# Moving a layer norm's statistics and its application between units of an attention pipeline

## The reference, cut to what matters

```python
x = x + attn(layernorm(x), wq, wk, wv, wo)   # x: (4, 256, 256), 4 sequences of 256 tokens
x = x + ffn(layernorm(x), W1, W2, W3)
# layernorm: (x - mean) / sqrt(var + 1e-5), over the last axis
# attn: 16 query heads, 4 key/value heads of 128, rotary embedding (rope) on q and k,
#       causal scores times a decay exp(-lambda_h * lag), no softmax, then wo
# ffn:  silu(x W1^T) * (x W3^T), Walsh-Hadamard transform over 1024 hidden, then W2
```

## Time and profile before

| | before |
|---|---|
| runs | 272.18 us median of 3 (272.09 to 272.81) |
| the profiled execution | 272.2 us, span of its instructions 270.4 us |
| mean granted TensorE clock | 0.998 |
| busy: PE / DVE / ACT / POOL | 263.1 / 205.5 / 168.0 / 146.1 us |

### The profile page before, as it was taken

One profiled execution on the slowest core, in us unless ns is written; L12 is line 12 of the kernel. 1 busy time (PEld: TensorE's weight loads), 2 busy tenths in 40 slices (PEclk: granted clock), 3 DMA queues, 4 the chain that ended last, 5 costly groups with the idle time before them and its releaser, 6 DMA issues.

```text
span 270.4 us, 4196 instructions
## 1 busy us (share of the span) xinstructions
PE 263.1 (97%) x1498; PEld 228.0 (84%) x1498; DVE 205.5 (76%) x331; ACT 168.0 (62%) x283; POOL 146.1 (54%) x106
## 2 busy tenths in 40 slices
PE   8999799999999999999999999999999999999995
PEld 6686678988889898888889889898888879988895
DVE  2799999999879897959899799795576983143333
ACT  2988977985798767556867768984353542043230
POOL 2306999988879467532795897899519200000000
PEclk9999999999999999999999999999999999999999
DMA  5595422220220000000010002200000000100002
GB/s 185 187 354 176 167 80 80 78 78 0 80 71 10 0 1 0 4 0 0 2 59 18 2 4 73 78 5 0 2 0 2 0 0 23 57 0 0 2 0 78
DMA packets 5491, 13.23 MB, mean 49 GB/s; under 512 B 608, under 2 KB 2272, under 8 KB 5472
## 3 DMA queue, kind: packets, MB, share of 16 engines
q1 hardware_dynamic: 5184, 12.65, 13.5%
q10 hardware_dynamic: 288, 0.33, 0.3%
HBM read 11.93 MB, written 1.05 MB: 48 GB/s over the span
## 4 chain that ended last, share of the span: by engine, by line
PE 79%; DVE 15%; issue 3%; ACT 2%; POOL 0%; DVEq 0%; POOLq 0%
PE bank L312 25%; PE bank L313 24%; PE bank L314 24%; PE bank L335 3%; DVE rope_b L973 2%; DVE bank L1000 2%; PE bank L330 2%; DVE p_lo L1005 2%; DVE rope_a L972 1%; DVE o_lo L1010 1%; DVE v_hid L959 1%; DVE rope_b L1024 1%; DVE w_lo L947 1%; DVE x_sb L1048 1%; DVE stats L904 1%
## 5 line engine op out<-in xcount | busy, mean ns | idle before, releaser
L807 POOL TENSOR_TENSOR qk<-rope_a,rope_b 128x512 f32<-128x512 f32 x37 | 50.6, 1371 | 24.8 <-DVE rope_b L973 24.5
L312 PE MATMUL bank<-xt_hi,w_hi 128*128 128x512 f32 x142 | 56.1, 395 | 0.2
L313 PE MATMUL bank<-xt_lo,w_hi 128*128 128x512 f32 x142 | 55.5, 391 | 0.0
L314 PE MATMUL bank<-xt_hi,w_lo 128*128 128x512 f32 x142 | 55.4, 390 | 0.0
L814 POOL TENSOR_TENSOR q_hid<-qk,q_hid 128x512 fp32r<-128x512 f32 x30 | 41.5, 1396 | 9.7 <-ACT q_hid L634 9.7
L973 DVE TENSOR_TENSOR rope_b<-rope_b,sin_sb 128x512 f32<-128x512 f32 x40 | 39.5, 988 | 0.0
L641 ACT ACTIVATE p_hi<-bank 128x512 fp32r<-128x512 f32 x48 | 28.6, 596 | 14.0 <-DVE bank L1000 13.5
L313 PE MATMUL bank<-w_lo,o_hi 128*128 128x256 f32 x128 | 36.2, 283 | 0.0
L314 PE MATMUL bank<-w_hi,o_lo 128*128 128x256 f32 x128 | 36.2, 283 | 0.0
L312 PE MATMUL bank<-w_hi,o_hi 128*128 128x256 f32 x128 | 36.1, 282 | 0.0
L972 DVE TENSOR_TENSOR rope_a<-bank,cos_sb 128x512 f32<-128x512 f32 x40 | 27.5, 687 | 10.7 <-ACT rope_b L629 9.9
(11 more groups left out here) (86 smaller groups left out, 607.9 us busy)
## 6 DMA issues: line engine op xcount, KB each, us to landing
w_raw<-in_w SPq DMA_DIRECT2D x6, 512.0 KB, 3.3
decay_sb<-in_decay SPq DMA_DIRECT2D x4, 512.0 KB, 5.3
w_raw<-in_wo SPq DMA_DIRECT2D x4, 512.0 KB, 4.6
w_raw<-in_wq SPq DMA_DIRECT2D x3, 512.0 KB, 3.3
out<-x_sb SPq DMA_DIRECT2D x8, 128.0 KB, 1.8
x_sb<-in_x SPq DMA_DIRECT2D x3, 256.0 KB, 6.9
w_raw<-in_wq SPq DMA_DIRECT2D x2, 256.0 KB, 5.6
w_raw<-in_wv SPq DMA_DIRECT2D x1, 512.0 KB, 6.0
```

The source lines that it names most:

```text
L312: pe.matmul(o, a_hi, b_hi, start=first, stop=False, skip_group_check=shared)
L313: pe.matmul(o, a_hi, b_lo, start=False, stop=False, skip_group_check=shared)
L314: return pe.matmul(o, a_lo, b_hi, start=False, stop=last, skip_group_check=shared)
L807: pool.tensor_tensor(qk[:, r % 2, :], rope_a[:, r % 2, :], rope_b[:, r % 2, :], ALU.add).then_inc(rope_sum_pool, 1)
```

## The change

The norm of half 1 moves. On DVE the first tile's statistics stand behind `low_o(3, 0)`, just before the loop; the other three, the four means and `add_eps` come at the end of unit 4; `norm_shift(1)` stands in unit 5 between `low_o(4, 1)` and `low_p(5, S_SECOND)`. On POOL `inverse_deviation(1)` is the first instruction of unit 5. On ACT the four applications leave the end of unit 4; two of them stand before `high_p(5, S_FIRST1)` in unit 5 and two behind it. PE's list is the same, and so is everything for the other three norms (`STATS_AT` gives units 8 to 10 what the formula gave them). The number of instructions doesn't change.

```diff
--- before.py
+++ after.py
@@ -98,6 +98,9 @@
 
     c, p = divmod(u, PAIRS)
     return [("X", c + 1, k) for k in range(KD)] if p == PAIRS - 3 else []
+
+
+STATS_AT = {4: (1, 2, 3), 8: (0,), 9: (1, 2), 10: (3,)}
 
 
 def unit_chunk(u):
@@ -759,16 +762,20 @@
                 for item in key(u - 1) if u else []:
                     high_rope(item)
                 fill(queries(u)[1:])
+                if u == 5:
+                    norm_apply(1, range(2))
                 high_p(u, S_FIRST1)
                 if u in (UNITS - 2, UNITS - 1):
                     silu(u - UNITS + 2)
                 fill(values(u)[2:3])
+                if u == 5:
+                    norm_apply(1, range(2, TT))
                 high_o(u, 0)
                 fill(values(u)[3:])
                 if unit_chunk(u) is not None:
                     high_weights(unit_chunk(u))
-                if u % PAIRS == 4:
-                    norm_apply(u // PAIRS + 1, range(TT))
+                if u == 12:
+                    norm_apply(2, range(TT))
             high_hid(0)
             high_hid(1)
             high_w2(0)
@@ -867,16 +874,17 @@
             rope_add(("K", 0, 2))
             low_rope(("Q", 0, 9))
             low_rope(("K", 0, 2))
-            inverse_deviation(1)
             rope_add(("Q", 0, 10))
             rope_add(("Q", 0, 11))
             low_weights(8)
             for u in range(FIRST_UNIT, UNITS):
                 if u:
                     before = queries(u - 1)
+                    if u == 5:
+                        inverse_deviation(1)
                     for item in before[:1]:
                         low_rope(item)
-                    if u % PAIRS == 3:
+                    if u == 11:
                         inverse_deviation(u // PAIRS + 1)
                     for item in key(u - 1):
                         rope_add(item)
@@ -1108,8 +1116,6 @@
             low_weights(5)
             low_o(0, 1)
             low_p(1, S_SECOND)
-            tile_stats(1, 0)
-            tile_mean(1, 0)
             low_p(1, S_FIRST1)
             rotate(("Q", 0, 6))
             low_o(1, 0)
@@ -1117,33 +1123,26 @@
             mask(2, S_FIRST0)
             mask(2, S_SECOND)
             low_p(2, S_FIRST0)
-            tile_stats(1, 1)
             low_o(1, 1)
             low_p(2, S_SECOND)
             mask(2, S_FIRST1)
             rotate(("Q", 0, 8))
             low_p(2, S_FIRST1)
-            tile_stats(1, 2)
             rotate(("Q", 0, 9))
             mask(3, S_FIRST0)
             low_o(2, 0)
             low_weights(7)
             mask(3, S_SECOND)
             rotate(("K", 0, 2))
-            tile_mean(1, 1)
-            tile_mean(1, 2)
             low_p(3, S_FIRST0)
             low_p(3, S_SECOND)
-            tile_stats(1, 3)
-            tile_mean(1, 3)
-            add_eps(1)
             mask(3, S_FIRST1)
             low_o(2, 1)
             rotate(("Q", 0, 10))
             rotate(("Q", 0, 11))
             low_p(3, S_FIRST1)
             low_o(3, 0)
-            norm_shift(1)
+            tile_stats(1, 0)
             for u in range(FIRST_UNIT, UNITS):
                 if u:
                     mask(u, S_FIRST0)
@@ -1151,6 +1150,8 @@
                     fill(key(u - 1) + turned(u - 1))
                     low_p(u, S_FIRST0)
                     low_o(u - 1, 1)
+                    if u == 5:
+                        norm_shift(1)
                     low_p(u, S_SECOND)
                 fill(values(u)[:1])
                 mask(u, S_FIRST1)
@@ -1167,13 +1168,12 @@
                 fill(values(u)[3:])
                 if unit_chunk(u) in LOW_ON_DVE:
                     low_weights(unit_chunk(u))
-                i, p = u // PAIRS + 1, u % PAIRS
-                for t in ((0,), (1, 2), (3,))[p] if p < 3 else ():
-                    tile_stats(i, t)
-                if p == 2:
-                    norm_variance(i)
-                if p == 3:
-                    norm_shift(i)
+                for t in STATS_AT.get(u, ()):
+                    tile_stats(u // PAIRS + 1, t)
+                if TT - 1 in STATS_AT.get(u, ()):
+                    norm_variance(u // PAIRS + 1)
+                if u == 11:
+                    norm_shift(2)
             low_hid(0)
             low_hid(1)
             low_w2(0)
```

## The result

The changed kernel took 273.88 us (median of 4 runs, 273.51 to 274.02) against 272.17 us before (4 runs): ratio 1.005, 95% interval 1.0031 to 1.0068. Run again later, beside other kernels, it took 273.93 us (7 runs) against 272.64 (29 runs): 1.0055, interval 1.0033 to 1.0076. A thirtieth run of the kernel before took 429.09 us, at a granted clock of 0.561, and is left out. The ratios are not the quotients of the two medians and can differ from them by some 0.001 (the quotient here is 1.0047). The forecast was 273.8.

The account below looks back on a forecast made before the run. TensorE, busy 97% of the span, was taken as the bound, so only its stalls count. A 2.1 us stall less a 0.49 gain gave +1.6 on 272.2 us: forecast 273.8, range 272.6 to 274.7.

Parts of the forecast that it names:

- Part one, first stall: PE's wait for `low_o(2,1)` ahead of `attend(3,0)` goes, as DVE loses norm work: 0.50 us gained.
- Part one, second stall: PE's wait ahead of `attend(3,1)` shrinks depending on DVE-POOL ties at two sine products; whole gain 0.29, 0.49 (taken) or 0.96.
- the case of 0.96: DVE wins both ties with POOL at the sine products of Q10 and Q11: whole gain of part one 0.96 us.
- Part two: Norm at unit 4's end: eps waits out POOL's `w_lo` to 78.5; the detour costs K3's chain 0.15 us.
- Part three: ACT's four applications in unit 5, before PE's turn (its transposes), delay `scores(6)` from 85.88 to 87.99: a 2.1 us stall.
- The sum: Whole kernel: 2.1 − 0.49 = +1.6 us on 272.2 us, forecast 273.8.
- (a): Rival, chance 0.07: ACT keeps up at the turn, only part one's gain shows, 0.3 to 1.0 us faster, about 271.7.
- (b): Rival, chance 0.15: small stall at the turn, 1.3 or 1.8, less a 0.96 gain, +0.35 to +0.8: 272.8.
- (c): Rival, chance 0.10: second stall ahead of the turn, `low_p(5, S_SECOND)` late behind `norm_shift`, adds 0.5 to 1: 274.6.
- (d): Rival, chance 0.03: PE's clock drops to 1.2 GHz for a stretch after the stall, another 2.1 us lost: 275.9.
- A sign that was badly set: At PE's turn: forecast wrong if the turn starts within 0.3 us of `attend(5,0)`'s end.

Follow-up runs that it names:

- split_only: The kernel before with only ACT's four applications moved to unit 5, DVE and POOL keeping the norm in units 1 to 3: 274.21 us, ratio 1.0067.
- late_means_eps: late_eps with two more means moved from in front of `low_p(3, S_FIRST0)` to behind `low_o(3, 0)`: 271.60 us, ratio 0.9978.
- late_eps: The kernel before; fourth tile's statistics, mean, `add_eps` and shift moved from unit 3's end to unit 4, the pow behind POOL's weights: 271.91 us, again 271.97 us.

## Why the prediction was right, step by step

- **Part one, first stall: right.** `low_o(2,1)` was due at 60.23 and stands at 60.29; 0.50 went.
- **Part one, second stall: right in mechanism, the middle value wrong.** I took 0.49, for DVE winning the first tie and losing the second. In both traces DVE won both, the case of 0.96 (`low_o(3,0)` at 64.47). But it is not the whole story: POOL, held by the winner, ended `low_rope(K2)` at 63.32, and `scores(4)` waited 0.3 for it. I had asked who waits for DVE when POOL is first, and not who waits for POOL when DVE is. The net is 0.64: `attend(3, 1)` starts 56.77 us behind the first projection instead of 57.34, and its first matmul is 0.07 shorter.
- **Part two: right.** Eps was to wait to 78.5 less the gain, and ended at 77.87; POOL's addition of K3 was to start at 81.6 less the gain, and started at 80.86. Eps took 1.16 us beside POOL, not 0.17, and ended 0.03 behind POOL's `w_lo`. Here the rule of the Trainium skill (SBUF — State Buffer, "SBUF: two separate sides") and the trace agree. The later kernels add 1.82 and 2.10 us for eps and 1.25 for the shift. The price of the detour was too high: I put 0.15 on it, and the swap of Q15 starts 0.66 us earlier than before (73.28 against 73.94 behind the first projection), which is the whole gain. The stall of 1.8 that I gave for an eps that isn't held is what split_only shows, 1.80.
- **Part three: right.** A stall of 2.1 was worked out, 1.96 measured. The pitch of 0.49 held in every variant; the tail of five transposes and its handover took 0.57 (86.63 to 87.20), not 0.6, and the first application began at 84.08, which is 84.72 in the times of the trace before (the gain of 0.64 added), not 84.84.
- **The sum.** 2.1 less 0.49 was +1.6; the traces give 1.96 less 0.64, +1.3. The measured medians differ by 1.71 and, the second time, by 1.27. That the first median fell within 0.1 us of the forecast is partly chance: both terms were off by some 0.15 in the same direction, and the spread between executions (4 runs each) made up for it.
- **The rivals.** (a) didn't happen, for the reason given: ACT's saving can't be carried past PE's projections. split_only shows it, with ACT waiting 0.83 and 0.97 us for PE; in the change it went mostly into the 1.57 us for the masks behind eps. (b) was too small: its stall of 1.3 to 1.8 with a gain of 0.96 gives at most +0.8, and 1.96 less 0.64 were measured. (c) didn't: `low_p(5)` was ready. (d) didn't: the window of the stall has the granted clock at 1.00.

```profile
84.00:88.00 4.00, 2.88 (x17) 1.97 (x16) 3.97 (x5) 3.97 (x9) 2.75 (x3) 1.00 0.01 2
```

- **A sign that was badly set.** I had written that I would be wrong if the turn started within 0.3 us of `attend(5, 0)`'s end. The row of its last matmul ends at 84.61 and the first transpose starts at 84.82, 0.21 later. By the letter the sign was there; but the first transposes need only the first tile, and the stall comes from the third and fourth. The sign should have been the start of `scores(6)`.

What stays open: what puts some executions of each kernel (from a quarter to two thirds of them) 0.5 us or more above its lowest time. The tie near 56 us is one candidate, but only 2 of 14 traces show it lost; the start, which differs by up to 0.9 us between traces, is another. Only one trace of the kernel before exists.

## What to carry to other kernels

When a step is moved down an engine's list, look for the last thing on that list that depends on the bottleneck engine and stands ahead of it: time saved before that point can't be carried past it, and each instruction behind it that the bottleneck has to wait for costs its pitch. Often it is cheaper to move the consumer: here 1.4 us of other matmuls in front of the transposes took back three quarters of the delay. A small instruction that needs a shared port is priced by what it may meet there, not by its own length, so give it a place where the other engine is idle or waits for it.

## What the runs showed of the hardware

- At level requests for the port that DVE and POOL share, either can be first: near 56 us DVE was first in 12 traces and POOL in 2, with starts 0.02 us apart or less. At the sine product of Q10, 0.16 us less on DVE's list decides it: DVE's 0.68 and POOL's 1.84 in one order (late_means_eps), 1.72 and 1.30 in the other (late_eps). Where POOL ended an instruction and had the next one ready, a waiting DVE went between them: in the kernel before a sine product asked at 83.45 while POOL was busy from 82.73 to 84.03, and ended at 84.58; POOL's next, of 83.99, took 1.74 us instead of 1.30.
- The statistics (line 904), which read one tile from SBUF, took 0.41 us beside a running POOL instruction, while eps and the shift on 128 x 4 numbers waited it out, up to 2.10 us for eps and 1.25 for the shift.
- Executions of one kernel aren't one number with noise. The same program had distances of 258.06 and 257.26 us, by one lost tie, and the start varied by up to 0.9 us between the traces of all kernels (first projection at 9.44 to 10.30 us), by 0.5 us between two of one kernel (late_eps).
